# Turning by VectorE's 32x32 blocks in place of TensorE transposes, in the two narrow attention layers of a four-layer network

## The reference

```python
def _L0_cond_ref(x, cond, ...):            # D = 256, H = 16, HD = 16
    h = _ada_ln(x, cond, Wln1, bln1)
    q, k, v = heads(h @ Wq + bq), heads(h @ Wk + bk), heads(h @ Wv + bv)
    scores = einsum('bhqd,bhkd->bhqk', q, k) / sqrt(HD)
    attn = softmax(scores, axis=-1)
    out = einsum('bhqk,bhkd->bhqd', attn, v)
    x = x + out.transpose(0, 2, 1, 3).reshape(B, L, D) @ Wo + bo
    h = _ada_ln(x, cond, Wln2, bln2)
    return x + gelu(h @ W1 + b1) @ W2 + b2

def _L2_cond_ref(x, c, padding_mask, ...): # the same, masked, and both residuals gated
    attn = where(mask, q @ k.T * HD ** -0.5, -1e9)
    x = x + gate_msa[:, None, :] * (softmax(attn) @ v @ proj_w.T + proj_b)
    return x + gate_mlp[:, None, :] * (gelu_tanh(h @ fc1_w.T + fc1_b) @ fc2_w.T + fc2_b)
```

## Time and profile before

| | |
|---|---|
| time, median of 3 runs (lowest to highest) | 5980.17 us (5980.14 to 5980.99) |
| span of the profiled execution | 5979.2 us |
| TensorE (PE) busy | 5638.8 us, 94% |
| VectorE (DVE) busy | 4312.5 us, 72% |
| ScalarE (ACT) busy | 4114.6 us, 69% |
| GpSimd (POOL) busy | 2806.3 us, 47% |
| first narrow layer, one batch after another | 100.8 us each |
| second narrow layer, one batch after another | 102.3 us each |
| wide layer, one batch after another | 182.0 us each |

### The profile page before, as it was taken

How to read it: one execution, slowest core, us unless ns; L and a number is a source line. 1 busy time by engine, 2 the same in 40 slices (tenths; PEclk the granted TensorE clock), 3 DMA queues, 4 the chain that set the end, 5 groups by cost and what they waited for, 6 DMA issues and landing times. The chain is left out here.

```text
span 5979.2 us, 76519 instructions
## 1 busy us (share of the span) xinstructions
PE 5638.8 (94%) x28360; PEld 2996.1 (50%) x28360; DVE 4312.5 (72%) x4700; ACT 4114.6 (69%) x6785; POOL 2806.3 (47%) x2193
## 2 busy tenths in 40 slices
PE   8999999999999998899998999999999999999998
PEld 5545445555555554454544444454444444444445
DVE  5767644434444435667675989989898998989898
ACT  3454545544455543545446989999898999989897
POOL 0000002322222221001012969969696987969697
PEclk8999999999999999999999999999999999999999
DMA  4323221000000004232332111020201102020200
GB/s 134 54 39 58 35 62 14 3 2 3 2 1 2 3 2 57 42 66 42 59 56 50 36 38 46 24 60 29 54 29 47 36 22 61 31 53 31 53 31 22
DMA packets 168740, 222.44 MB, mean 37 GB/s; under 512 B 37169, under 2 KB 104074, under 8 KB 168114
## 3 DMA queue, kind: packets, MB, share of 16 engines
q1 hardware_dynamic: 168370, 217.55, 16.9%
HBM read 152.90 MB, written 30.49 MB: 31 GB/s over the span
## 5 line engine op out<-in xcount | busy, mean ns | idle before, releaser
L2524 DVE TENSOR_TENSOR_SCAN l__h<-l__decay,psum 128x1024 f32<-128x1024 f32 x1024 | 2250.3, 2267 | 53.8 <-ACT l__decay L1972 16.0
L2490 POOL TENSOR_TENSOR l__hc<-l__h,l__c_rep 128x1024 f32<-128x1024 f32 x1016 | 2011.5, 2010 | 92.8 <-DVE l__h L2524 67.2
L1972 ACT ACTIVATE l__decay<-l__dt_rep,l__a_neg 128x511 f32<-128x511 f32 x2048 | 1339.5, 708 | 9.1 <-DVE l__h L2524 9.0
L1982 PEld LDWEIGHTS psum<-ident,l__dtx_B 128*128 128x128 f32 x8192 | 882.7, 141 | 850.6 <-DVE l__h L2524 491.6
L2608 PE MATMUL psum<-l__hc,l__gather 128*64 128x512 f32 x4096 | 1104.6, 617 | 140.0 <-POOL l__hc L2490 139.4
L1982 PE MATMUL psum<-ident,l__dtx_B 128*128 128x128 f32 x8192 | 1119.3, 280 | 35.4 <-DVE l__h L2524 16.2
L1956 ACT ACTIVATE l__dtx_B<-l__dtx_T,l__b_T 128x512 f32<-128x512 f32 x1664 | 1103.5, 709 | 5.8 <-PE psum L1982 3.7
L691 DVE TENSOR_REDUCE l__row_max<-psum 128x1 f32<-128x512 f32 x1024 | 651.0, 683 | 221.4 <-PE psum L706 220.7
L1411 POOL TENSOR_SCALAR l__probs<-l__probs,l__rec 128x512 f32<-128x512 f32 x512 | 348.7, 694 | 886.3 <-DVE l__rec L1407 885.0
L199 POOL TENSOR_SCALAR l__ln_var_eps<-l__ln_mean_var 128x4 f32<-128x4 f32 x56 | 16.1, 287 | 1488.3 <-DVE l__ln_mean_var L185 1488.3
L1039 ACT ACTIVATE l__probs<-psum 128x1024 f32<-128x1024 f32 x512 | 503.7, 1023 | 207.8 <-PE psum L1111 203.2
(11 more groups left out here) (189 smaller groups left out, 6484.2 us busy)
## 6 DMA issues: line engine op xcount, KB each, us to landing
l__c_rep<-l__c_dram SPq DMA_DIRECT2D x512, 128.0 KB, 2.9
l__dt_rep<-l__dt SPq DMA_DIRECT2D x128, 256.0 KB, 5.0
l__parts_dram<-l__parts SPq DMA_DIRECT2D x64, 384.0 KB, 3.4
l__q_stack<-l__parts_dram SPq DMA_DIRECT2D x192, 128.0 KB, 6.3
l__k_stack<-l__parts_dram SPq DMA_DIRECT2D x192, 128.0 KB, 8.8
l__w<-in_l_w SPq DMA_DIRECT2D x6, 1024.0 KB, 7.6
l__gate_rows<-l__gates_dram SPq DMA_DIRECT2D x24, 256.0 KB, 3.2
in_mod_w<-in_mod_w SPq DMA_DIRECT2D x1, 4608.0 KB, 17.6
```

The source lines that it names most:

```text
L1972: nc.scalar.activation(decay[:, i % DECAYS, s, 1:T], dt_rep[:, w, c, s, 1:T], ACT.Exp, scale=a_neg[:, g, c, s:s + 1]).then_inc(S["decay"], 1)
L1982: last = nc.tensor.transpose(bx_psum(i)[:, s, t * P:(t + 1) * P], dtx_B[:, (k + 1) % 2, t, 2 * c + s, :, :].rearrange("p j d -> p (j d)"), ...
L2490: nc.gpsimd.tensor_tensor(hc[:, i % HCS, :, :], h[:, i % HS, :, :], c_of(i), ALU.mult).then_inc(S["hc"], 1)
L2524: nc.vector.tensor_tensor_scan(both(h[:, i % HS, :, :]), both(decay[:, i % DECAYS, :, :]), both(bx_psum(i)), 0.0, ALU.mult, ALU.add).then_ ...
```

## The change

Both turns go to VectorE's transpose, which transposes each block of 32x32. The maxima are stored by tile number, split into two bf16 columns side by side, and four transposes of [32, 32] for a group put them on 32 rows of 128 columns, from where DMAs of 16 rows each (every second partition) fill the two rows of the q stack. A group of `oT` is turned in one VectorE transpose of [128, 512], so that a query's 16 outputs and its sum lie on one partition. It is normalised there into a compact layout of two groups in one chunk, and one transpose turns a chunk back. `wo` then has two full chunks in place of four half-empty ones, filled by eight DMAs, with no clearing. TensorE has no transposes left for these, and `project_out` 8 multiplications in place of 16.

```diff
+        def max_high(dve, gg, done, taken):
+            dve.wait_ge(*S.at("max_taken", taken))
+            if done > 1 or S.batch:
+                dve.wait_ge(*S.at("max_turned", GH * (done - 1)))
+            nc.vector.tensor_scalar(mcol[:, :, 0], mx[:, gg, :], -1.0, None, ALU.mult).then_inc(S["max_high"], 1)
+
+        def max_low(dve, gg, done):
+            dve.wait_ge(*S.at("max_high", done))
+            nc.vector.scalar_tensor_tensor(mcol[:, :, 1], mx[:, gg, :], -1.0, mcol[:, :, 0],
+                                           ALU.mult, ALU.subtract).then_inc(S["max_low"], 1)
+
+        def max_turn(dve, done):
+            dve.wait_ge(*S.at("max_low", done))
...
+            cols = mcol[:, :, :].rearrange("p n k -> p (n k)")
+            for a in range(GH):
+                nc.vector.transpose(mrow[:, a, :], cols[2 * GT * a:2 * GT * (a + 1), :]).then_inc(S["max_turned"], 1)
+
+        def early_max(dve, n, done, taken):
+            take_max(dve, n, taken + n + 1)
+            if n == GT:
+                max_high(dve, 0, done, taken + GT)
+            if n == GT + 1:
+                max_low(dve, 0, done)
+            if n == GT + 2:
+                max_turn(dve, done)
...
             for k in range(2):
                 sp.dma_start(qs[k_max + k:k_max + k + 1, gg * GH:(gg + 1) * GH, :],
-                             mrow[:, k, :]).then_inc(S["max_rows"], 16)
+                             mrow[k::2, :, :]).then_inc(S["max_rows"], 16)
...
+            def turn(gg):
+                dve.wait_ge(*S.at("oT", gg + 1))
+                if gg >= 2:
+                    dve.wait_ge(*S.at("normed", gg - 1))
+                nc.vector.transpose(o_q[:, gg % 2, :, :].rearrange("p b r -> p (b r)"),
+                                    oT[:, gg, :]).then_inc(S["turned"], 1)
+
             def normalise(gg):
+                dve.wait_ge(*S.at("turned", gg + 1))
+                nc.vector.reciprocal(rec[:, gg, :], o_q[:, gg % 2, :, HD]).then_inc(S["rec"], 1)
+                dve.wait_ge(*S.at("rec", gg + 1))
+                nc.vector.tensor_tensor(o_n[:, gg // 2, :, gg % 2, :], o_q[:, gg % 2, :, 0:HD],
+                                        rec[:, gg, :].unsqueeze(2).broadcast_to([P, QB, HD]),
+                                        ALU.mult).then_inc(S["normed"], 1)
+
+            def turn_back(c):
+                dve.wait_ge(*S.at("normed", 2 * c + 2))
+                nc.vector.transpose(oT[:, c, :], o_n[:, c, :, :, :].rearrange("p b k d -> p (b k d)"))\
+                    .then_inc(S["oT_norm"], 1)
...
-                if n % GT == 3 and n > LEAD:
-                    make_max_rows(dve, slot_bank(rows_slot(n // GT - 1)), n // GT - 1)
+                gg = n // GT - 1
+                if n > LEAD and n % GT == 0:
+                    max_high(dve, gg, gg, GT * (gg + 1) - LEAD)
+                if n > LEAD and n % GT == 1:
+                    max_low(dve, gg, gg)
+                if n > LEAD and n % GT == 2:
+                    max_turn(dve, gg)
...
-            for gg in range(NG - 1):
-                invert_sums(gg)
-            spread_rec(slice(0, NG - 1))
-            for gg in range(NG - 1):
-                normalise(gg)
-            invert_sums(NG - 1)
-            spread_rec(slice(NG - 1, NG))
-            normalise(NG - 1)
+            for c in range(DC):
+                for gg in (2 * c, 2 * c + 1):
+                    turn(gg)
+                    normalise(gg)
+                turn_back(c)
...
-            project_out(0, range(NG - 1))
-            pe.wait_ge(*S.at("rec", 1))
-            sums(NG - 1)
-            for t in range(1, TT):
-                project_out(t, range(NG - 1))
-            spread(NG - 1)
+            for t in range(TT):
+                project_out(t, 0)
+            pe.wait_ge(*S.at("max_taken", LATER))
+            if F:
+                pe.wait_ge(*F.S.at("hT", DC))
             if more:
+                pe.wait_ge(*S.at("oT", NG))
                 project_qk(pe, 0)
-            pe.wait_ge(*S.at("oT_norm", NG))
+            pe.wait_ge(*S.at("oT_norm", DC))
             for t in range(TT):
-                last = project_out(t, (NG - 1,))
+                last = project_out(t, 1)
...
-            sp.wait_ge(*S.at("zeroed", 1))
-            wo_v = io[tag + "wo"].rearrange("(g j d) n -> j d g n", j=GH, d=HD)
+            wo_v = io[tag + "wo"].rearrange("(c k j d) n -> j k d c n", k=2, j=GH, d=HD)
             for j in range(GH):
-                sp.dma_start(wo[j * 2 * HD:j * 2 * HD + HD, :, :], wo_v[j]).then_inc(S["late"], 16)
+                for k in range(2):
+                    row = (2 * j + k) * HD
+                    sp.dma_start(wo[row:row + HD, :, :], wo_v[j, k]).then_inc(S["late"], 16)
```

More of the change, by code:

```diff
@@ L539, in narrow_attention_layer @@
         LATE_RING = (6, 0, 1)
[L540 to L543, removed]
+        max_bank = lambda n: bank[n % RING0 if n < LEAD else LATE_RING[(n - LEAD) % len(LATE_RING)]]
         pair = lambda n: psum[:, 4 - 2 * (n // 2 % 2):6 - 2 * (n // 2 % 2), :]
[L545 to L546 removed]
         S = Semaphores(pool_of, LN_SEMS + [
[L548 removed]
+            "load", "ones", "ones_in", "late", "cur", "gate_out", "gate_rows", "qk_filled", "v_filled", "qk", "part1", "rest", "part2",
             "part3", "v", "parts_out0", "parts_out1", "parts_out2", "parts_out3", "stacks0", "stacks1", "valid_in",
[L550 to L551 removed]
+            "mask_in", "max_filled", "max_taken", "max_high", "max_low", "max_turned", "max_rows", "st_filled",
+            "exp", "av", "oT", "turned", "rec", "normed", "oT_norm", "y_filled", "res", "up_filled", "gelu",
             "down_filled", "mlp_out", "mlp_res"], {
@@ L714, in early_scores @@
             scores(pe, n)
[L716 to L719, removed]
         def stacks_ready(pe):
@@ L1083, in tensor_batch @@
             more, more2, x_b = about(b)
-            def slot_free(pe, slot):
-                of = slot - len(LATE_RING)
-                rows = sum(rows_slot(gg) < of for gg in range(1, NG))
-                if rows + 1 < NG and rows_slot(rows + 1) == of:
-                    pe.wait_ge(*S.at("max_part2", rows + 1))
-                elif of >= 0 or S.batch:
-                    pe.wait_ge(*S.at("max_taken", of - rows + 1))
             def late_scores(n):
@@ L1127, in values, with project_out @@
                 last.then_inc(S["av"], 1)
-            def sums(gg):
-                pe.wait_ge(*S.at("oT", gg + 1))
-                for t in range(TT):
-                    last = nc.tensor.transpose(bank[SUM_BANKS[gg]][:, t * P:(t + 1) * P], oT[:, gg, t * P:(t + 1) * P],
-                                               ident[:, :])
-                last.then_inc(S["sum_filled"], 1)
-            def spread(gg):
-                pe.wait_ge(*S.at("rec_rep", 1 if gg < NG - 1 else 2))
-                if gg >= 2:
-                    pe.wait_ge(*S.at("oT_norm", gg - 1))
-                for t in range(TT):
-                    rows = rec_rep[:, gg, t, :, :].rearrange("p j r -> p (j r)")
-                    last = nc.tensor.transpose(bank[gg % 2][:, t * P:(t + 1) * P], rows, ident[:, :])
-                last.then_inc(S["head_filled"], 1)
-            def project_out(t, groups):
-                for gg in groups:
-                    last = nc.tensor.matmul(psum[:, 2 + t, 0:D], oT[:, gg, t * P:(t + 1) * P], wo[:, gg, :],
-                                            start=(gg == 0), stop=(gg == NG - 1))
-                return last
+            def project_out(t, c):
+                return nc.tensor.matmul(psum[:, 2 + t, 0:D], oT[:, c, t * P:(t + 1) * P], wo[:, c, :],
+                                        start=(c == 0), stop=(c == DC - 1))
             for n in range(LEAD, TILES + GT + LEAD):
```

97 lines of the change are left out of this document (25 added, 72 removed).

## The result

The changed kernel takes 5843.03 us, median of 4 runs (5840.61 to 5849.43), against 5980.16 us before on the same chip (5978.07 to 5980.99). The ratio is 0.977, with a 95% interval from 0.9756 to 0.9784: 2.3% faster. The forecast was 5842, in a range of 5816 to 5874.

The account below looks back on a forecast made before the run. TensorE, busy 94% of the span, was taken as the bound; 4.4 + 2.3 + 1.76 + 0.3 = 8.76 us a batch, 140.2 over 16, less 1.5 once, gives 138.7 off: 5842 us, range 5816 to 5874.

Parts of the forecast that it names:

- end of the batch: First output projection to next batch's second q/k projection: 9.61 us becomes 5.2, VectorE's chain hidden; 4.4 us won a batch.
- last 24 tiles: Last 24 key-side tiles: TensorE loses 3.5 us, but ScalarE's exps are close behind; 2.3 us won, between 1.5 and 3.0.
- groups 1 and 2: TensorE loses 0.44 us of transposes and 0.44 of waiting for L700 in each; 1.76 us won a batch.
- group 0: In the down-projection, VectorE's time counts: 0.6 to 0.95 us replaces 1.35; 0.3 us won, between 0 and 0.6.
- Price of what goes: TensorE's removed transposes cost 0.11 us each by the trace, not the mean of 272 ns; 48 make 5.3 us a batch.
- rival 2: Wide VectorE transposes at 1.4 us, plus small 0.3 or rows 1 us later: 5868 to 5874 us; chance 0.20.
- the rule in the prediction: VectorE's four small transposes, starting in different 32-partition groups, don't overlap: about 0.25 us more a group, up to 4 in all.
- with waits for L1039: Sign for the last 24 tiles: ScalarE nearly without gaps and TensorE waiting for L1039 would show ScalarE's bound is right.
- rival 3: Small-piece DMAs land rows later; 3.7 us later eats the 8.8 us; chance 0.06 shared with no effect and smaller gains.
- What happens once: First batch of second narrow layer loses 2.7 us, last batches 1.0, openings win 2.2: 1.5 us lost in all.
- The opening of the first layer: VectorE's two operations ahead of the barrier move into the tiles: 1.35 us less, 1.1 taken.
- The last batch of the second narrow layer: Each layer's last batch has no q projection to cover VectorE's chain: about 0.5 us lost each.

Follow-up runs that it names:

- turning twice: Changed kernel with group 3's turn and the second chunk's turn back each done twice, doubles thrown away: 5860.08 us, ratio 0.9794.
- half the exps: Changed kernel with the last 12 exps of each batch (24 tiles) taken of half the columns only: 5822.47 us, ratio 0.9729.
- the maxima alone: Kernel before with only the maxima turned by VectorE, heads' outputs as before: 5939.89 us, ratio 0.9929.
- the outputs alone: Kernel before with only the heads' outputs turned by VectorE and two full chunks of wo, maxima as before: 5889.29 us, ratio 0.9846.
- projecting early: Changed kernel with half of the output projection's first chunk moved ahead of the last block of values: 5844.8 us, ratio 0.9771.

## Why the prediction was right, step by step

| term, us a batch | forecast | measured |
|---|---|---|
| end of the batch | 4.4 | 9.61 - 5.27 = 4.34 |
| last 24 tiles | 2.3 | 15.83 - 13.65 = 2.18 |
| groups 1 and 2 | 1.76 | 25.90 - 24.28 = 1.62 |
| group 0 | 0.3 | 20.80 - 20.48 = 0.32 |
| sum | 8.76 | 8.46 |

The stage of group 0 runs from VectorE's first early tile to its copy of `cur` (262.31 to 283.11 before, 245.22 to 265.70 after), that of groups 1 and 2 from there to the exps at 309.01 and 289.98.

*Price of what goes.* Counting TensorE's transposes by the distance between starts, 0.11 us, held: the sum came out 0.30 us too high of 8.76, where by the mean of 272 ns in the earlier trace rows the 48 transposes alone would be worth 13.1 us.

*End of the batch.* Right, and for the reason given: the chain was forecast with 0.4 us to spare and had 0.57, and turning twice found 0.6. VectorE's wide transpose at 0.71 us decided against rival 2. That the 0.69 taken for it came so near is luck: it was the price of another operation, and the rows allowed 0.43 to 1.4.

*Group 0.* Right, and for the reason given, VectorE's time. The small transposes don't overlap, as the rule in the prediction has it, and cost 0.82 us of that time. But the two operations ahead of them cost only 0.07 and 0.08, being overlapped: 0.97 us in place of 275.33 - 274.02 = 1.31. Of rival 2's other half, small ones of 0.3 us or later rows, neither came.

*Last 24 tiles.* Right: forecast 2.3 by ScalarE's pace against 3.5 by TensorE's, measured 2.18; with half the exps 1.63 more. One sign was read too simply: TensorE "with waits for L1039" was expected as a row of them. There are two, 0.2 and 0.6 us; for the rest the two engines alternate over two pairs of banks, and ScalarE has 1.73 us of gaps, TensorE 0.91.

*Rows landing later (rival 3).* No wait of TensorE for these DMAs is left in the steady batches, so 16 pieces of 256 bytes cost nothing that can be seen. They don't land later: in the changed kernel both DMAs have landed a median of 2.25 us after the first is issued (64 groups), and for group 3 at 292.76, which is 2.3 us after VectorE had the rows at 290.43. Before, the trace has no landings, but TensorE went on 2.3 us after the issue and 2.4 after VectorE had them.

*What happens once.* Here a step failed: "Four more cost 1.8 us, and what TensorE wins ahead of that wait (0.9 us) is lost in it". That batch was 10.90 us shorter (124.57 to 113.67), 2.4 more than the 8.46 of its neighbours, not 2.7 less. In the seven traces with eight DMAs it is 19.0 to 22.5 us longer than its neighbours, where the forecast has 22.3 + 2.7 = 25.0; with four it is 22.3 in the kernel before and 25.1 with the maxima alone. The price of 0.44 us for one more issue was right (0.42), but it isn't added: the first issue behind the column writes took 6.71 us in place of 11.18, so four took 12.59 us and the eight of the changed kernel 9.98. That the wait comes from the column writes is shown, since with these moved it is gone; why it is shorter with smaller pieces of `wo` behind them is not, and stays open. The opening of the first layer won 0.5 us instead of 1.1 (VectorE's first copy of `cur` starts at 80.85, not at 81.36); but in the other traces with the new opening it starts at 80.66 to 84.13, so one trace can't show that gain.

The last batch of the second narrow layer, up to its down-projection, won 6.2 us instead of 8.76 - 0.3 - 0.5 = 8.0. In it the up-projection took 1.29 us longer (windows before and after; the columns are those of the earlier trace rows):

```profile
3181.94:3198.41 16.47, 15.69 (x32) 6.58 (x32) 12.62 (x20) 6.77 (x10) 0.11 (x1) 0.90 0.00 0
3043.28:3061.04 17.76, 16.99 (x32) 7.10 (x32) 12.63 (x20) 6.78 (x10) 0.11 (x1) 0.83 0.00 0
```

The mean granted clock of this stretch (part of it at 2.4 and part at 1.2 GHz) goes with it in all twelve traces: 16.2 to 16.5 us at 0.90 to 0.91 in six, 17.4 to 17.8 at 0.83 to 0.85 in six, and time by clock is 14.7 to 14.8 us in each. So these 1.3 us are the clock's. It does not follow the change: the maxima alone have 17.75 us, the outputs alone 16.35. What decides it stays open.

*The total.* 16 x 8.46 = 135.4 us in the sum above, 136.4 between the two spans and 137.1 between the medians, against 138.7 forecast. The total came out closer than its terms deserve, and that is luck: the steady batches brought 4.8 us less than forecast, and what happens once, forecast as a loss of 1.5 us, made it up in part.

## What to carry to other kernels

Move work off the engine that is full even when it costs more elsewhere, but price it there by the distance between starts, and read for each stage which engine ends next: here the same kind of edit was worth its full TensorE time at the end of the batch and six tenths of it (2.18 of 3.5 us) beside ScalarE's exps. When a stall is filled, ask what the moved work was covering: projecting early won 0.48 us and gave 0.46 back, most of it because it was the cover of the next chain. Two edits that shorten the same wait don't add up. What a single trace shows of something that happens once is to be checked against the other traces in which it recurs: the first batch's wait moved by up to 2.8 us with nothing of it changed. The largest gain for a few lines was found beside the change: 17 us (5843.03 to 5826.34) for moving a few slow writes out of the way of a queue whose next entries someone waits for.

## What the runs showed of the hardware that was not expected

- VectorE's transpose of [128, 512] f32 takes 0.71 us from SBUF and 0.72 from PSUM. At [32, 32] bf16, 1/16 of the columns, it still takes 0.198 us.
- Changing the kind of work on TensorE was not free here: four records of the output projection next to blocks of values take 0.96 to 1.06 us, where eight in a row take 1.73 to 1.83.
- After a wait of 17.6 us TensorE was granted half its clock for 4.3 us more.
- The same up-projection took 16.2 to 16.5 us or 17.4 to 17.8 us, by a mean granted clock of 0.90 to 0.91 or 0.83 to 0.85, in kernels that differ little.
- An issue of `wo` took up to 11.18 us behind the column writes and at most 0.54 with these moved. In one trace each, eight DMAs of half the size took 13.42 us to issue there and four 12.59; over nine traces it was 4.8 to 13.4 us for eight and 8.7 to 12.6 for four, and TensorE waited less with eight (17.0 to 19.8 us against 20.5 to 21.7).
